# Attention head pairs with v's two halves in one stationary tile: four value passes per head for six, parts summed off TensorE

## The reference

```
qkv = norm(x) @ W_qkv ; q, k, v = split(qkv, 3)          # 16 heads x 64
attn = softmax(einsum('bqhd,bkhd->bhqk', q, k) * 64**-0.5)
out = einsum('bhqk,bkhd->bqhd', attn, v).reshape(16, 256, 1024)
x = x + gate * (out @ W_out + b_out)
```

## Time and profile before

| | |
|---|---|
| median of three runs | 1785.5 us |
| profiled execution, its own time | 1785.71 us |
| its span (first to last instruction) | 1783.9 us |
| PE busy | 1685.8 us (95%) |
| DVE / ACT / POOL busy | 1174.3 / 1131.1 / 1005.2 us (66 / 63 / 56%) |
| mean granted TensorE clock | 0.971 of full speed |
| phase 2: start of its first and of its last copy of transposed probabilities | 270.3 and 1024.9 us |

### The profile page before, as it was taken

The page is one execution under the profiler, slowest core; times in us unless marked ns, Lnnn a source line. Parts: engine busy times, 40 slices in busy tenths (PEclk is TensorE's granted clock), DMA queues, the critical chain, the costliest instruction groups (busy, mean ns, idle before and its releaser), DMA issues.

```text
span 1783.9 us, 38293 instructions
## 1 busy us (share of the span) xinstructions
PE 1685.8 (95%) x13763; PEld 1529.5 (86%) x13763; DVE 1174.3 (66%) x2830; ACT 1131.1 (63%) x2828; POOL 1005.2 (56%) x1141
## 2 busy tenths in 40 slices
PE   4887989999999999999999889999999979989997
PEld 2557979999999999999999779998888879979997
DVE  4775757777777777777777654446776658864442
ACT  3544746767777767777677565556676657766663
POOL 1554756776676777767676623334565648842223
PEclk7998999999999999999999989999999989989999
DMA  8112310000000000000000011110111112210111
GB/s 305 53 50 73 95 45 11 11 11 10 2 11 11 10 11 11 11 11 10 11 11 11 1 23 40 31 31 29 48 55 45 55 22 51 46 51 26 47 49 47
DMA packets 110975, 65.98 MB, mean 37 GB/s; under 512 B 81530, under 2 KB 92788, under 8 KB 110788
## 3 DMA queue, kind: packets, MB, share of 16 engines
q1 hardware_dynamic: 110788, 63.54, 13.1%
HBM read 59.06 MB, written 4.46 MB: 36 GB/s over the span
## 4 chain that ended last, share of the span: by engine, by line
PE 85%; issue 5%; DVE 3%; POOL 3%; ACT 2%; DMA 1%; POOLq 0%; SPq 0%; DVEq 0%; ACTq 0%
PE bank L252 25%; PE bank L253 23%; PE bank L254 23%; PE bank L967 5%; PE bank L1023 5%; PE bank L380 3%; PE bank L440 1%; ACT nThi L393 1%; ACT bank L393 1%; DVE stats L316 1%; POOL x L627 1%; POOL xb L793 0%; DVE xn L339 0%; POOL rstd L331 0%; PE bank L1318 0%
## 5 line engine op out<-in xcount | busy, mean ns | idle before, releaser
L1005 POOL TENSOR_SCALAR prob<-prob,rinv 128x256 f32<-128x256 f32 x512 | 465.0, 927 | 212.7 <-DVE rinv L999 212.7
L573 ACT ACTIVATE hh<-bank,vecs 128x512 fp32r<-128x512 f32 x240 | 167.6, 698 | 283.7 <-PE bank L254 283.4
L579 DVE TENSOR_TENSOR hl<-bank,hh 128x512 fp32r<-128x512 f32 x240 | 163.9, 685 | 216.3 <-ACT bank L573 215.8
L990 ACT ACTIVATE prob<-bank,nmax 128x256 f32<-128x256 f32 x512 | 238.9, 477 | 4.2 <-DVE nmax L980 4.1
L252 PE MATMUL bank<-WBhi,hl 128*128 128x256 f32 x768 | 218.1, 284 | 10.9 <-DVE upd L610 10.9
L1033 ACT ACTIVATE pthi<-bank 128x512 fp32r<-128x512 f32 x256 | 139.2, 595 | 135.7 <-PE bank L1023 135.7
L253 PE MATMUL bank<-WBlo,hh 128*128 128x256 f32 x768 | 217.3, 283 | 0.0
L254 PE MATMUL bank<-WBhi,hh 128*128 128x256 f32 x768 | 217.2, 283 | 0.0
L1038 DVE TENSOR_TENSOR ptlo<-bank,pthi 128x512 fp32r<-128x512 f32 x256 | 175.4, 686 | 23.0 <-ACT pthi L1033 23.0
L980 DVE TENSOR_REDUCE nmax<-bank 128x2 f32<-128x512 f32 x256 | 175.1, 685 | 19.9 <-PE bank L967 19.0
L252 PE MATMUL bank<-aThi,WAlo 128*128 128x256 f32 x576 | 177.6, 308 | 7.6 <-POOLq L242 7.6
(11 more groups left out here) (164 smaller groups left out, 5167.6 us busy)
## 6 DMA issues: line engine op xcount, KB each, us to landing
gates<-gate_scratch SPq DMA_DIRECT2D x96, 256.0 KB, 3.6
agate<-gate_scratch SPq DMA_DIRECT2D x32, 256.0 KB, 3.7
stage<-in_L_cond_W SPq DMA_DIRECT2D x64, 64.0 KB, 2.3
out<-x SPq DMA_DIRECT2D x16, 256.0 KB, 2.2
adaw<-in_L_cond_Wc SPq DMA_DIRECT2D x1, 3072.0 KB, 17.6
stage<-in_L_cond_W_qkv SPq DMA_DIRECT2D x8, 384.0 KB, 3.4
x<-in_x SPq DMA_DIRECT2D x1, 2560.0 KB, 16.9
stage<-in_L_cond_ff_w SPq DMA_DIRECT2D x32, 64.0 KB, 2.1
```

The lines of the kernel that those rows point to most:

```text
L573: last = act.activation(dst[:, :], U_BANKS[r][:, :], ACTF[p], bias=vecs[:, at:at + 1])
L579: dve.tensor_tensor(hl[r][:, :], U_BANKS[r][:, :], hh[r][:, :].bitcast(F32), ALU.subtract).then_inc(h_lo, 1)
L990: last = act.activation(prob[h % 4][:, q, :], SB_[h % 2][:, q * SEQ:(q + 1) * SEQ], ACT.Exp, bias=nmax[h % 4][:, q:q + 1], accum_out=rsum[ ...
L1005: last = pool.tensor_scalar(prob[h % 4][:, q, :], prob[h % 4][:, q, :], rinv[h % 4][:, q:q + 1], None, ALU.mult)
```

## The change

1. **v in one tile.** The tiles vhi and vlo become one tile `vv`, with 256 columns for a pair: hi, lo of the even head, then lo, hi of the odd head. The stationary tile of a head is its hi and lo side by side, without zeros. Two passes per chunk (pt's low half, pt's high half) instead of three: four per head, eight per pair. The product of low by low, which was left out before, is now in the sum.
2. **The parts summed off PE.** Each head now has a whole [128, 256] half of bank 7: 64 rows with the product by vhi ("main") and 64 with the product by vlo ("rest"). ACT copies each head's rest across to the main's rows in a tile `oc` (`o_read`, two instructions of [64, 256]). DVE adds main and rest into `of` (two instructions), then copies `of` to oThi, from SBUF to SBUF (`o_add`). POOL subtracts for oTlo (`o_rest`). Both halves of bank 7 are now taken by one pair, so the next pair's value products wait for the two adds (`o_sum`).
3. **Maxima and 1/sum by pair.** Banks 2 and 3 are one tensor; one reduction gives the maxima of both heads (128 by 1024 elements to four columns), and one reciprocal serves both. It comes ahead of both `pt_rest`. The exponentials of a pair's first head wait for the pair's maxima, and the weighing for both heads' sums.
4. **v's halves** are written by one instruction of 512 columns on ACT and one on DVE instead of two of 256 on each; the zeroing on POOL at the start of the phase goes.

The core of the diff:

```diff
-        VP = 3 * DH
-        vv = [sb(f"v{k}", [P, TPB, PAIRS * VP], F32R, att) for k in ("hi", "lo")]
+        VP = 4 * DH
+        vv = sb("vv", [P, TPB, PAIRS * VP], F32R, att)
+        of = [sb(f"of{i}", [P, SEQ], scope=att) for i in range(2)]
+        oc = sb("oc", [P, SEQ], scope=att)
...
-        def score_max(dve, h):
-            dve.wait_ge(s_mm, h + 1)
+        def score_max(dve, n):
+            dve.wait_ge(s_mm, 2 * n + 2)
+            if n >= 2:
+                dve.wait_ge(exp_ready, 2 * n - 2)
+            dve.tensor_reduce(nmax[n % 2][:, :], s_banks[:, :, :].rearrange("p h (q k) -> p (h q) k", q=TPB), AX_X, ALU.max,
+                              negate=True).then_inc(nmax_ready, 2)
...
         def score_exp(act, h):
-            act.wait_ge(nmax_ready, h + 1)
+            act.wait_ge(nmax_ready, h - h % 2 + 2)
...
         def head_values(pe, own, h):
             if h % 2 == 0 and H:
-                pe.wait_ge(o_lo, H // 2)
+                pe.wait_ge(o_sum, H)
             for c in range(TPB):
-                last = split3(pe, OB[:, i * SEQ:(i + 1) * SEQ], [m[:, c, at:at + P] for m in vv],
-                              [m[:, c * SEQ:(c + 1) * SEQ] for m in pt[h % 2]],
-                              c == 0 and h % 2 == 0, c == TPB - 1 and h % 2 == 1)
+                for m in (1, 0):
+                    last = pe.matmul(OB[:, h % 2 * SEQ:(h % 2 + 1) * SEQ], vv[:, c, h * P:(h + 1) * P],
+                                     pt[h % 2][m][:, c * SEQ:(c + 1) * SEQ],
+                                     start=c == 0 and m == 1, stop=c == TPB - 1 and m == 0, skip_group_check=True)
...
+        def o_read(act, pair):
+            act.wait_ge(pv_mm, 2 * pair + 2)
+            if pair:
+                act.wait_ge(o_sum, 2 * pair)
+            for j in range(2):
+                main, rest, cols = o_halves(j)
+                act.activation(oc[main, :], OB[rest, cols], ACT.Copy).then_inc(o_corr, 1)
+        def o_add(dve, pair, i):
+            for j in range(2):
+                main, _, cols = o_halves(j)
+                dve.wait_ge(o_corr, 2 * pair + 2)
+                dve.tensor_tensor(of[i][main, :], OB[main, cols], oc[main, :], ALU.add).then_inc(o_sum, 1)
+            dve.wait_ge(o_sum, 2 * pair + 2)
+            dve.tensor_copy(oT[i][0][:, :], of[i][:, :]).then_inc(o_hi, 1)
+        def o_rest(pool, pair, i):
+            pool.wait_ge(o_hi, pair + 1)
+            pool.tensor_tensor(oT[i][1][:, :], of[i][:, :], oT[i][0][:, :].bitcast(F32),
+                               ALU.subtract).then_inc(o_lo, 1)
...
         def mh_vector(dve, b, j):
             if n + 1 < PERIODS:
-                for h in range(2):
-                    prob_inverse(dve, 2 * n + 2 + h)
+                prob_inverse(dve, n + 1)
             if n:
-                o_rest(dve, n - 1, (n - 1) % 2)
+                o_add(dve, n - 1, (n - 1) % 2)
+            if n + 2 < PERIODS:
+                score_max(dve, n + 2)
             for h in range(2):
-                if n + 2 < PERIODS:
-                    score_max(dve, 2 * n + 4 + h)
                 pt_rest(dve, 2 * n + h)
...
         def mh_gpsimd(pool, b, j):
             if n + 1 < PERIODS:
                 prob_weigh(pool, 2 * n + 2)
+            if n:
+                o_rest(pool, n - 1, (n - 1) % 2)
```

More of the change, by code:

```diff
@@ L163, in bass_cond_blocks @@
         smax = [sb(f"smax{i}", [P, TPB], scope=att) for i in range(1)]
-        nmax = [sb(f"nmax{i}", [P, TPB], scope=att) for i in range(4)]
-        rsum = [sb(f"rsum{i}", [P, TPB], scope=att) for i in range(4)]
-        rinv = [sb(f"rinv{i}", [P, TPB], scope=att) for i in range(4)]
+        nmax = [sb(f"nmax{i}", [P, 2 * TPB], scope=att) for i in range(2)]
+        rsum = [sb(f"rsum{i}", [P, 2 * TPB], scope=att) for i in range(2)]
+        rinv = [sb(f"rinv{i}", [P, 2 * TPB], scope=att) for i in range(2)]
         front_a, front_b = DC * HID[0] + HID[0] // P * D, DC * HID[1] + HID[1] // P * D
@@ L193, in bass_cond_blocks @@
         be = sb("be", [P, 2, DC, BATCH])
-        bank = [ctx.enter_context(nc.psum_tensor(f"bank{i}", [P, 512], F32)) for i in range(8)]
+        bank = [ctx.enter_context(nc.psum_tensor(f"bank{i}", [P, 512], F32)) for i in range(2)]
+        s_banks = ctx.enter_context(nc.psum_tensor("s_banks", [P, 2, 512], F32))
+        bank += [s_banks[:, i, :] for i in range(2)]
+        bank += [ctx.enter_context(nc.psum_tensor(f"bank{i}", [P, 512], F32)) for i in range(4, 8)]
         T_BANKS = [bank[7], bank[6]]
@@ L938, in proj_scalar @@
                 heads4 = src[:, :].rearrange("p (j h d) -> p j h d", h=2, d=DH)
-                for h, dst in enumerate(v_heads(vv[0], tile, half)):
-                    last = act.activation(dst, heads4[:, :, h, :], ACT.Copy)
-                last.then_inc(proj_hi, 1)
+                act.activation(v_heads(tile, half)[0], heads4, ACT.Copy).then_inc(proj_hi, 1)
         def proj_vector(dve, own, what):
@@ L953, in proj_vector @@
                 heads4 = src[:, :].rearrange("p (j h d) -> p j h d", h=2, d=DH)
-                for h, (hi, lo) in enumerate(zip(v_heads(vv[0], tile, half), v_heads(vv[1], tile, half))):
-                    last = dve.tensor_tensor(lo, heads4[:, :, h, :], hi.bitcast(F32), ALU.subtract)
-                last.then_inc(proj_lo, 1)
+                hi, lo = v_heads(tile, half)
+                dve.tensor_tensor(lo, heads4, hi.bitcast(F32), ALU.subtract).then_inc(proj_lo, 1)
         def pair_scores(pe, n):
@@ L1054, in head_values, with o_halves @@
             last.then_inc(pv_mm, 1)
-        def o_read(act, pair, i):
+        def o_halves(j):
+            main, rest = slice(j * DH, (j + 1) * DH), slice((1 - j) * DH, (2 - j) * DH)
+            return main, rest, slice(j * SEQ, (j + 1) * SEQ)
+        def o_read(act, pair):
             act.wait_ge(pv_mm, 2 * pair + 2)
-            if pair >= 2:
-                act.wait_ge(out_mm, pair - 1)
-            act.activation(oT[i][0][:, :], OB[:, i * SEQ:(i + 1) * SEQ], ACT.Copy).then_inc(o_hi, 1)
@@ L1166, in mh_scalar @@
             if n:
-                o_read(act, n - 1, (n - 1) % 2)
+                o_read(act, n - 1)
             for h in range(2):
@@ L1183, in mh_scalar @@
             if n == PERIODS - 1:
-                o_read(act, n, n % 2)
+                o_read(act, n)
         def mh_vector(dve, b, j):
@@ L1237, in mh_gpsimd @@
             if n == PERIODS - 1:
+                o_rest(pool, n, n % 2)
                 res_add(pool, b, b)
@@ L1249, in mh_start @@
             if name == "gpsimd":
-                for m in vv:
-                    pads = m[:, :, :].bitcast(F32).rearrange("p t (j w) -> p t j w", w=VP)[:, :, :, DH:2 * DH]
-                    for k in range(TPB):
-                        last = eng.memset(pads[:, k, :, :], 0.0)
-                last.then_inc(zeros, 1)
                 for h in range(2):
@@ L1260, in head_pair @@
             def head_pair(n):
-                for h in (2 * n, 2 * n + 1):
-                    if name == "vector":
-                        score_max(eng, h)
-                    if name == "scalar":
+                if name == "vector":
+                    score_max(eng, n)
+                if name == "scalar":
+                    for h in (2 * n, 2 * n + 1):
                         score_exp(eng, h)
@@ L1276, in mh_start @@
             if name == "vector":
-                for h in range(2):
-                    prob_inverse(eng, h)
+                prob_inverse(eng, 0)
             head_pair(1)
@@ L1293, in bass_cond_blocks @@
         qk1, kk1 = qk
-        vv1 = [[m[:, 0, i * ROWW:(i + 1) * ROWW] for m in vv] for i in range(2)]
+        vv1 = [[vv[:, k, i * ROWW:(i + 1) * ROWW] for k in range(2)] for i in range(2)]
         a1 = [[m[:, :, :] for m in aT],
-              [m[:, 1, 0:ROWW].rearrange("p (c r) -> p c r", c=DC) for m in vv]]
+              [vv[:, k, 2 * ROWW:3 * ROWW].rearrange("p (c r) -> p c r", c=DC) for k in range(2)]]
         def sh_exp(act, b):
@@ L1349, in sh_scale @@
                 dve.wait_ge(prob_ready1, b - 1)
-            dve.reciprocal(rinv[0][:, :], rsum[0][:, :]).then_inc(rinv_ready, 1)
+            dve.reciprocal(rinv[0][:, 0:TPB], rsum[0][:, 0:TPB]).then_inc(rinv_ready, 1)
             dve.wait_ge(rinv_ready, H0 + b + 1)
```

46 lines of the change are left out of this document (20 added, 26 removed).

## The result

The changed kernel takes 1854.2 us (median of four runs, 1852.51 to 1854.59); the kernel before, beside it, 1784.3 (four runs). The ratio is 1.0386, 95% interval 1.0371 to 1.0402: 3.9% slower. The forecast was 1846 us with a range from 1812 to 1868.

What follows compares the result with a forecast made beforehand. DVE and ACT's loop, not PE, bounds the attention: eight periods of 5.58 plus 5.94 and worse collisions make 51.4 us a batch against 47.43. Over 15.5 batches, less 1.9, +60 on 1785.7: 1846 us, range 1812 to 1868.

Steps and rivals of the forecast that it cites:

- the loop: DVE and ACT's fixed cycle per attention period, from row maxima to next row maxima: 5.58 us against PE's 4.68.
- PE stays the bound: Rival: PE still bounds the attention, 61 us gained in part or whole, 1725 to 1780 us; chance 0.05.
- the cancelling: Rival: in the attention, shorter PE time and the longer loop cancel, 1780 to 1791 us; chance of no change 0.04.
- The wait put down to POOL: In the attention, PE's wait may be put down to POOL (chain 5.23 us against 5.58), though the loop sets the period.
- Wrong: Signs against the forecast: periods of 4.7 to 5.1 us, maxima under 1.0, copies at 0.29, PE waiting on oTlo, lower clock.
- the adds: DVE's two 256-column adds of main and rest in each attention period: 0.74 us, plus 0.04 until the copy.
- ACT's second o_read: ACT's second read of a pair's rest, per period: costs nothing, in time ACT waits for the transposes (1.05 us idle).
- The collision: DVE's copy into oThi waits until POOL's current weighing instruction ends: 0.12 us more per period, 5.58 for 5.46.
- the two "worse" collisions: Twice per batch the copy meets POOL worse: 0.33 us more in period 1, 0.46 in period 5 or 6.
- The extras: Other DVE and ACT work put into the loop per batch (vlo, aupd, norm statistics, xn, next rows, casts): 5.94 us.
- The last four periods: End of the attention, nothing projected: the loop loses 1.24, PE's saving of 4 x 0.48 shows; 1.9 us taken off.
- one ring beside the loop: In each attention period, POOL's weighings from 1/sum, then transposes to the next reciprocal: 5.23 us against 5.58.

Runs made afterwards that it cites:

- e5: The changed kernel with two value passes per head for four (the product with pt's low half left out): 1857.3 us, ratio 1.0401.
- e12: The changed kernel with six value passes per head for four (the product of pt's low half taken twice): 1866.0 us, ratio 1.0452.
- e11: The changed kernel with a second, useless copy of `of` on DVE in front of the maxima: 1880.3 us, ratio 1.0537.
- e3: The changed kernel with the copy to oThi on ACT, behind pt_read, instead of on DVE: 1815.1 us, ratio 1.0166.
- e2: The changed kernel with the maxima again one instruction per head, the reciprocal still by pair: 1820.3 us, ratio 1.0198.
- e6: The changed kernel with half of POOL's weighing left out (one of two instructions per head): 1848.3 us, ratio 1.0350.
- e9: The changed kernel with a pair's output projection one period later, POOL's oTlo and the residual's update moved along: 1850.9 us, ratio 1.0376.
- e8: The changed kernel with both adds of a pair on rows 0 to 63, the odd head's share of the output left out: 1835.9 us, ratio 1.0282.
- e4: The changed kernel with maxima by head and the copy to oThi on ACT, both together: 1809.1 us, ratio 1.0133.
- e1: The kernel before with part 3 of the change alone (maxima and 1/sum by pair): 1778.1 us, ratio 0.9960.
- e10: The kernel before with the reciprocals by pair alone, maxima still by head: 1776.9 us, ratio 0.9961.

## Why the prediction was right

**What bounds it, right.** PE no longer does. Taking passes off gave nothing (e5), adding four per pair back cost 12 us (e12), adding 0.18 us and more to each turn of the loop cost nearly all of it (e11), taking 0.33 or 0.53 off gave 39 and 34 us (e3, e2). The rival "PE stays the bound" is out, and with it the cancelling.

**The wait put down to POOL, right.** I had said that PE's waits might bear POOL's name though the loop sets the period. They do (88.6 us), and e6 and e9 take POOL's work or that wait away for 6 and 2 us. But under "Wrong" I had also named PE's waits on oTlo as the sign that POOL's place decides. That sign came, and it misled: the prediction holds both readings, and only the experiments chose.

**The loop's length, 5.58 forecast, 5.83 measured.** Maxima right (1.23), exponentials and hand-overs right within 0.08. Undersized: the adds by 0.13, since I took them to follow each other like two vlo (held, e8); and the way to them by 0.20, since I put ACT's second o_read at nothing. It is hidden where ACT waits for the transposes, as I said, but DVE waits for it.

**The collision, right in kind and too large.** Copies ended 0.14 to 0.15 us after POOL's weighing, as the earlier trace rows had it: of 104 copies in batches 1 to 13, 39 were clearly lengthened (0.36 to 0.37 us), always those of the same three places in a batch, and ended 0.145 after the weighing that they had started in. But they start later than I had it, by the 0.13 and 0.20 just named, when little of a weighing is left: 0.324 us on the mean for an undisturbed 0.294, 0.03 in place of 0.12. In e8, where they start earlier, it is 0.413. The group of that cast in the attention (mean ns of one behind the comma):

```profile
L1085 DVE CAST oThi<-of 128x256 fp32r<-128x256 f32 x126 | 40.8, 324 | 4.3
```

That the copy still takes 0.33 to the maxima is the hold. My sum was right there by luck, for a wrong reason. Nor did the two "worse" collisions come: in period 1 the copy ran its 0.295 us 0.40 us into a weighing, unhindered, once in each batch; in e11 the second copy right behind it did wait, to 0.148 us after that weighing's end. The rule of the Trainium skill that the prediction names (SBUF — State Buffer, "SBUF: two separate sides") has no room for that one, and I can't explain it; the profile's spans on POOL are rough.

**The batch, 51.4 forecast, 51.74 measured, by two errors that nearly cancel.** The mechanism is the one forecast; that the number came so close is in part luck. Eight loops are 46.6 for 44.6, and what else is put into them 5.1 for 6.7 (5.94 and the worse collisions 0.79). The extras are smaller partly because a vlo between qkhi and the adds covers the wait for ACT. This period shows it:

```profile
657.93 0.17 DVE L1005 RECIPROCAL rinv<-rsum 128x4 f32<-128x4 f32 x1
658.01 0.84 DVE L1081 TENSOR_TENSOR of<-bank,oc 64x256 f32<-64x256 f32 x2
658.89 0.37 DVE L1085 CAST oThi<-of 128x256 fp32r<-128x256 f32 x1
659.29 1.23 DVE L986 TENSOR_REDUCE nmax<-s_banks 128x4 f32<-128x1024 f32 x1
```

**The last four periods, wrong.** I took 1.9 us off; the last batch lost 5.2, of which 5.0 lie in its last four periods (from pthi to pthi 6.21, 7.18, 9.08 and 7.09 us for 5.16, 5.02, 9.41 and 4.94 before). That is a step that failed in sign. It makes 6.9 of the 9 us between the forecast's +60 and the 68.9 of the traces. Without projections nothing stands between a pair's value passes and its output projection; the new path over ACT's copy, the adds, DVE's copy and POOL's subtraction is longer than the old one over two instructions, and lies bare. PE, ACT and DVE there:

```profile
1072.34 0.39 PE L257 MATMUL bank<-WAhi,oTlo 128*128 128x256 f32 x1 [2.43 <-POOL oTlo L1090]
...
1088.51 0.58 PE L257 MATMUL bank<-WAhi,oTlo 128*128 128x256 f32 x1 [2.33 <-POOL oTlo L1090]
```

```profile
1074.69 0.78 ACT L1072 ACTIVATE oc<-bank 64x256 f32<-64x256 f32 x2 [0.58 <-PE bank L1055]
```

```profile
1075.58 0.87 DVE L1081 TENSOR_TENSOR of<-bank,oc 64x256 f32<-64x256 f32 x2 [1.20 <-ACT oc L1072]
```

The clock has a part in it. The last batch of the changed kernel and that of the kernel before as windows (granted clock behind the last bracket):

```profile
1045.30:1093.33 48.03, 35.36 (x331) 31.41 (x332) 33.41 (x70) 27.39 (x82) 35.05 (x41) 0.87 0.01 1
```

```profile
981.60:1024.41 42.81, 36.78 (x359) 33.41 (x360) 28.77 (x68) 24.70 (x77) 29.26 (x34) 0.92 0.01 2
```

Some 13 us at the lower level in the one, 7 in the other; how much of the 5.2 us that is I didn't separate. The path has a part of its own: e9, with 10 us at the lower level there, took 2.7 us off this batch by moving the projection.

**The second ring, not foreseen.** I had priced one ring beside the loop, over POOL's weighings and the transposes (5.23 us), but not the one over oTlo, the output projection and the value passes. The loop was ahead of it by little: e4 took 0.86 us off the loop and found the ring over oTlo 0.2 us behind. So the loop's terms price an addition nearly right (e11) and overprice a removal (e2, half).

**Signs that I had named.** They came as follows: batch within 50 to 53, q-k periods 5.8 for 5.6, PE's busy share 87% for 85%, ACT idle 1.12 us before the first exponential for 0.7, maxima 1.2; copies 0.29 to 0.41, half of them at 0.29 to 0.30, where I had wanted 0.3 to 0.9. Of the signs of being wrong, PE's waits on oTlo came, as said above, and a lower clock in the last batch alone.

## What to carry to other kernels

When the bounding engine gets less work, sum the period of every ring that other engines close among themselves, from start to start of real hand-overs, and compare each with the new floor; work on an engine that is 70% busy may be free (e1) or paid almost in full (e11), and the room in its ring says which. Follow the new path also where its cover is missing, at the end of a phase. And a wait that names an engine is tested by making that engine's work smaller or moving what waits: where the time doesn't move, the engine was only the last in a row.

## What the hardware showed that I had not expected

- Two DVE instructions of 64 x 256 on rows 0 to 63 and then 64 to 127 follow at 0.436 us, on the same rows at 0.331; the next instruction that reads PSUM from row 0 is held once more, 0.11 us (e8).
- PE was granted the lower clock level within the attention, ahead of its last batch, for 58 us with two passes (e5) and for 27 us in e9, in the changed kernel for none; ahead of the stretch shown for e5 PE had been busy for 1.66 of 3.4 us. In e5 less work on PE so made what remained slower, by some 8 us (an estimate, see e5).
- The edit of e10, one reciprocal of 128 x 4 in place of two of 128 x 2 with the tiles of two heads in one, made the kernel 0.4% faster, though PE was busy for 47.43 of 47.43 us in a batch before it. More than half of the gain lies behind the attention; the cause is open.
